# A recommender tower on one core: the first table rows on ScalarE's DMA queue, a later W2, a table-by-table low round in pass 1, and earlier holds for the gathers

## The reference

```python
e = jnp.stack([tbl_f[ids[:, f]] for f in range(26)], axis=1)           # 512 x 26 x 128
combined = jnp.concatenate([dense_features[:, None, :], e], axis=1)    # 512 x 27 x 128
interactions = jnp.einsum('bnd,bmd->bnm', combined, combined)
z = jnp.concatenate([dense_features, interactions[:, TRIU_I, TRIU_J]], axis=1)
h = jnp.concatenate([z, dense_features], axis=1)                       # 607 inputs
h = jnp.maximum(h @ W_top1 + b_top1, 0.0)                              # 512
h = jnp.maximum(h @ W_top2 + b_top2, 0.0)                              # 256
y = h @ W_top3                                                         # 512 x 1
```

## Time and profile before

| | |
|---|---|
| median of 3 runs | 121.35 us (120.82 to 123.39) |
| the profiled execution: its own time | 120.99 us |
| its span (first to last instruction) | 118.9 us |
| around the span | 2.09 us |
| PE busy, share of the span | 108.5 us, 91% |
| DVE, ACT, POOL busy | 85.0, 78.0, 57.3 us |

### The profile page before, as it was taken

How to read it: one execution, slowest core, us unless ns; L and a number is a source line. 1 busy time by engine, 2 the same in 40 slices (tenths; PEclk the granted TensorE clock), 3 DMA queues, 4 the chain that set the end, 5 groups by cost and what they waited for, 6 DMA issues and landing times.

```text
span 118.9 us, 2701 instructions
## 1 busy us (share of the span) xinstructions
PE 108.5 (91%) x1068; PEld 93.2 (78%) x1068; DVE 85.0 (71%) x171; ACT 78.0 (66%) x147; POOL 57.3 (48%) x66
## 2 busy tenths in 40 slices
PE   0079999999999999899999999999899999999993
PEld 0056787888888858558898999999789988999890
DVE  5779889999999957499959599582604981197002
ACT  4187838999999388599587699477504790178020
POOL 3777877787877777477740071078501700000000
PEclk9999999999999999999999999999999999999999
DMA  3899999692796924871210001001100000000000
GB/s 94 240 364 397 380 387 375 176 358 66 169 327 190 368 73 131 282 318 43 69 47 0 6 22 22 6 22 47 50 0 6 22 22 6 0 6 3 0 0 1
DMA packets 5582, 15.14 MB, mean 127 GB/s; under 512 B 1473, under 2 KB 1729, under 8 KB 5442
## 3 DMA queue, kind: packets, MB, share of 16 engines
q1 hardware_dynamic: 3890, 11.80, 28.0%
q0 software_dynamic: 1536, 3.15, 9.6%
q10 hardware_dynamic: 144, 0.02, 0.2%
HBM read 14.97 MB, written 0.00 MB: 126 GB/s over the span
## 4 chain that ended last, share of the span: by engine, by line
PE 70%; DMA 13%; ACT 8%; issue 3%; another core or an unknown queue 2%; DVE 1%; SPq 1%; ACTq 0%
PE dots_ps L712 13%; DMA table_raw<-picked_tables 13%; PE acc_ps L741 12%; PE dots_ps L628 10%; PE dots_ps L618 8%; PE turn_ps L757 5%; PE turn_ps L678 4%; PE acc_ps L651 3%; PE acc_ps L653 3%; PE acc_ps L732 3%; PE acc_ps L618 3%; PE acc_ps L628 3%; ACT z L382 2%; ACT cols L382 2%
## 5 line engine op out<-in xcount | busy, mean ns | idle before, releaser
L341 POOL DMA_INDIRECT rows<-tbl,ids_sb x48 | 53.5, 1114 | 16.6 <-issue 11.9
L515 DVE TENSOR_SCALAR onehot<-ids_row,row_number 128x1024 fp32r<-128x1024 int16 x49 | 33.6, 753 | 4.4 <-PE acc_ps L628 2.3
L359 DVE COPY z<-dots_ps 30x128 f32<-30x128 f32 (+5 forms) x80 | 21.0, 263 | 9.6 <-PE dots_ps L712 7.1
L382 ACT ACTIVATE z<-dots_ps 30x128 f32<-30x128 f32 (+5 forms) x80 | 19.7, 247 | 8.9 <-PE dots_ps L712 7.7
L382 ACT ACTIVATE table_hi<-table_raw 128x1024 fp32r<-128x1024 f32 (+1 forms) x16 | 15.2, 973 | 8.8 <-DMA table_raw<-picked_tables 6.8
L618 PE MATMUL acc_ps<-onehot,table_hi 128*128 128x512 f32 x52 | 14.4, 424 | 7.0 <-ACT table_hi L382 6.8
L618 PEld LDWEIGHTS acc_ps<-onehot,table_hi 128*128 128x128 f32 x52 | 10.2, 204 | 10.2 <-issue 6.8
L528 DVE TENSOR_TENSOR table_lo<-table_raw,table_hi 128x1024 fp32r<-128x1024 f32 (+1 forms) x16 | 17.1, 1114 | 1.2 <-ACT table_hi L382 1.2
L712 PEld LDWEIGHTS dots_ps<-cols 128*64 128x64 f32 x512 | 15.4, 138 | 1.1 <-issue 0.8
L712 PE MATMUL dots_ps<-cols 128*64 128x52 f32 x512 | 16.2, 222 | 0.0
L741 PE MATMUL acc_ps<-z,table_raw 128*128 128x128 f32 x128 | 15.3, 277 | 0.0
(11 more groups left out here) (48 smaller groups left out, 104.2 us busy)
## 6 DMA issues: line engine op xcount, KB each, us to landing
table_raw<-picked_tables SPq DMA_DIRECT2D x14, 512.0 KB
ids_row<-ids_picked SPq DMA_DIRECT2D x7, 256.0 KB
table_raw<-w SPq DMA_DIRECT2D x1, 1536.0 KB
rows<-tbl,ids_sb POOLq DMA_INDIRECT x48
w_sb<-w SPq DMA_DIRECT2D x1, 512.0 KB
table_raw<-picked_tables SPq DMA_DIRECT2D x2, 128.0 KB
dense_sb<-dense SPq DMA_DIRECT2D x1, 256.0 KB
ids_sb<-ids ACTq DMA_DIRECT2D x1, 24.0 KB, 2.5
```

The lines of the kernel that those rows point to most:

```text
L341: nc.gpsimd.indirect_dma_start(rows[:, t % GATHER_RING, n, :], None, tables[GATHERED[n]][:, :], index).then_inc(rows_in[t][g], 16)
L359: last = copy(z[QUAD * q:QUAD * q + rows_of, t % 2, :, QUAD * s + b0:QUAD * s + b1], src.rearrange("i b c -> i c b"))
L382: return nc.scalar.activation(dst, src, ACT.Copy)
L515: nc.vector.tensor_scalar(onehot[:, c], ids_row[:, pair % IDS_RING], row_number[first_row][:, c:c + 1], None, ALU.is_equal).then_inc(oneho ...
```

## The change

1. The two table loads of pass 0 go from SP's queue to ACT's, behind the ids of the gathers; SP's queue begins with ids row 0 and the tables of pass 1.
2. W2 and the last weights are issued behind W1 at the end of SP's list, and no longer behind the dense features near its start.
3. The memset of the unused columns of `cols` goes from DVE to Pool, ahead of Pool's first gather.
4. `lo_ready` counts once for each table, no longer once for each pass; all its waits are doubled. `LO_PIECE` goes, which alters no instruction.
5. In pass 1 PE's low round runs first over the eight chunks of table 0, as soon as that table's low part is there, and then over the eight of table 1; `chunk_done` is counted in the second half alone. In the other passes the two matmuls of a chunk stay together.
6. Pool's constants: the holds on `hi_used` stand at k = 17, 22, 27, 32, 37 (same counts 4, 5, 6, 7, 7), the memsets begin at k = 38, the pauses for `dots(0)`, `dots(1)`, `dots(2)` at k = 38, 40, 45, and `LANDED` follows.

```diff
-FREE_GATHERS = 20
+FIRST_FULL = 1
+FREE_GATHERS = 17
 GATHERS_A_PASS = 5
-LATE_GATHER = 39
+LATE_GATHER = 38
-PAUSES = {39: 0, 41: 1, 46: 2}
-LANDED = {0: 39, 1: 41, 2: 46}
+PAUSES = {38: 0, 40: 1, 45: 2}
+LANDED = {0: 38, 1: 40, 2: 45}
...
             load_ids_row(0)
-            load_tables(0)
-            load_tables(1)
+            load_tables(sp, 1)
             load_ids_row(1)
-            load_tables(2)
+            load_tables(sp, 2)
             sp.dma_start(dense_sb[:], dense).then_inc(dense_in, 16)
-            sp.dma_start(w2_sb[:], w2).then_inc(w2_in, 16)
-            sp.dma_start(last_sb[:], last_weights).then_inc(small_in, 16)
             for pair in range(IDS_RING, PAIRS):
                 p = FIRST_PASS[pair]
                 if p >= PASS_RING:
-                    sp.wait_ge(lo_ready, p - PASS_RING + 1)
-                    load_tables(p)
+                    sp.wait_ge(lo_ready, 2 * (p - PASS_RING + 1))
+                    load_tables(sp, p)
...
-            sp.wait_ge(lo_ready, NP - 1)
+            sp.wait_ge(lo_ready, 2 * (NP - 1))
             sp.dma_start(w1_sb, w1).then_inc(w1_in, 16)
+            sp.dma_start(w2_sb[:], w2).then_inc(w2_in, 16)
+            sp.dma_start(last_sb[:], last_weights).then_inc(small_in, 16)
...
+            nc.gpsimd.memset(cols[:, :, len(SLOT_NODE):SLOTS], 0.0).then_inc(cleared, 1)
             pool.wait_ge(ids_in, 16)
...
             act.dma_start(ids_sb[:], ids).then_inc(ids_in, 16)
+            load_tables(act, 0)
...
                     act.wait_ge(hi_used, p - 1)
-                    act.wait_ge(lo_ready, p - 1)
+                    act.wait_ge(lo_ready, 2 * (p - 1))
...
-            nc.vector.memset(cols[:, :, len(SLOT_NODE):SLOTS], 0.0).then_inc(cleared, 1)
...
                 for i in range(2):
-                    for c0 in range(0, n, LO_PIECE):
-                        part = slice(c0, min(c0 + LO_PIECE, n))
-                        last = nc.vector.tensor_tensor(table_lo[:, p % 2, i, part], table_raw[:, slot + i, part],
-                                                       table_hi[:, p % 2, i, part], ALU.subtract)
-                last.then_inc(lo_ready, 1)
+                    nc.vector.tensor_tensor(table_lo[:, p % 2, i, 0:n], table_raw[:, slot + i, 0:n],
+                                            table_hi[:, p % 2, i, 0:n], ALU.subtract).then_inc(lo_ready, 1)
...
-                pe.wait_ge(lo_ready, p + 1)
-                for c in ORDER[p]:
-                    for i in range(2):
-                        last = nc.tensor.matmul(sums[i], table_lo[:, p % 2, i, c, :], onehot[:, c, i, :],
-                                                start=False, stop=last_one and c == ORDER[p][-1])
-                    last.then_inc(chunk_done, 1)
+                def low(i, c):
+                    return nc.tensor.matmul(sums[i], table_lo[:, p % 2, i, c, :], onehot[:, c, i, :],
+                                            start=False, stop=last_one and c == ORDER[p][-1])
+
+                if p == FIRST_FULL:
+                    pe.wait_ge(lo_ready, 2 * p + 1)
+                    for c in ORDER[p]:
+                        low(0, c)
+                    pe.wait_ge(lo_ready, 2 * p + 2)
+                    for c in ORDER[p]:
+                        low(1, c).then_inc(chunk_done, 1)
+                else:
+                    pe.wait_ge(lo_ready, 2 * p + 2)
+                    for c in ORDER[p]:
+                        low(0, c)
+                        low(1, c).then_inc(chunk_done, 1)
```

More of the change, by code:

```diff
@@ L55 @@
 FIRST_PASS = [min(p for p in range(NP) if PASSES[p][0] == pair) for pair in range(PAIRS)]
-LO_PIECE = 8
 GATHERED = [f for f in range(NUM_TABLES) if f not in PICKED]
@@ L271, in build, with load_tables @@
         block = ctx.enter_context(nc.Block())
+        def load_tables(queue, p):
+            n = CHUNKS_OF[p]
+            for i in range(2):
+                slot = raw_slot(p) + i
+                r0 = 2 * P * CHUNKS_BEFORE[p] + i * P * n
+                src = picked_tables[r0:r0 + P * n].rearrange("(p c) d -> p c d", c=n)
+                queue.dma_start(table_raw[:, slot, 0:n], src).then_inc(table_in[slot], 16)
         @block.sync
@@ L276, in load_ids_row @@
                 sp.dma_start(ids_row[:, pair % IDS_RING], ids_picked[pair]).then_inc(ids_row_in[pair % IDS_RING], 16)
-            def load_tables(p):
-                n = CHUNKS_OF[p]
-                for i in range(2):
-                    slot = raw_slot(p) + i
-                    r0 = 2 * P * CHUNKS_BEFORE[p] + i * P * n
-                    src = picked_tables[r0:r0 + P * n].rearrange("(p c) d -> p c d", c=n)
-                    sp.dma_start(table_raw[:, slot, 0:n], src).then_inc(table_in[slot], 16)
             load_ids_row(0)
-            load_tables(0)
-            load_tables(1)
+            load_tables(sp, 1)
             load_ids_row(1)
-            load_tables(2)
+            load_tables(sp, 2)
             sp.dma_start(dense_sb[:], dense).then_inc(dense_in, 16)
-            sp.dma_start(w2_sb[:], w2).then_inc(w2_in, 16)
-            sp.dma_start(last_sb[:], last_weights).then_inc(small_in, 16)
             for pair in range(IDS_RING, PAIRS):
```

## The result

| | median, us | runs |
|---|---|---|
| before | 121.66 | 4 (120.82 to 123.39) |
| changed | 124.69 | 4 (123.57 to 125.64) |

The ratio is 1.0242, with an interval of 1.0127 to 1.0357: slower clear of noise, while the interval leaves open whether by more than 2 percent. All ratios and intervals here leave out the executions that were more than 1.5 percent above the fastest of their kernel, the medians do not. The forecast was 121.9, the range ended at 123.8. The profiled execution took 124.65 us, with a span of 122.9 against 118.9.

What follows compares the result with a forecast made beforehand. PE was taken as the bound, except for a load at the start. Span 118.9 + 0.55 (X) + 0.1 + 0.35 = 119.9, with 2.09 around it 122.0; forecast 121.9 us, range 119.4 to 123.8.

Steps and rivals of the forecast that it cites:

- late counts: Unexplained waits of DVE (2.3 us) and ACT (2.0) for PE's low-round counts, 36 to 56 us; carried unchanged.
- Rival 2: Pass 0 loads land no earlier and ACT's queue holds pass 1's copies: T 14.3, X +1.45, time 123.4 us; chance 0.15.
- T: End of PE's high round of pass 1, where its low round starts: 13.4 us forecast in place of 14.46.
- the split: Pass 1's table-by-table low round: first count 1.6 us later, one-hots of pass 2 at T + 2.44, X 0.55 later.
- X: End of DVE's low parts of pass 2, through which start gains reach the end: 22.85 us forecast against 22.31.
- DVE idle for over 2 us: Sign at the start: DVE idle this long ahead of the one-hots of pass 2, which start at 15.85 us.
- PE idle for 1 us ahead of its low round of pass 2: Sign: PE waits about 1 us for X, its low round of pass 2 starting near 23.1 us against 22.56.
- the second load of pass 0: On ACT's queue, forecast to land at 5.0 us, bounds 4.3 to 6.2, in place of about 6.25.
- rival 3: Late counts are accidental and the new holds remove them: -2.5 us, time 119.5, or 118.3 with rival 1; chance 0.15.
- The waits of the earlier trace: DVE's 2.3 us and ACT's 2.0 on PE's counts, 36 to 56 us; a change in size would show the forecast wrong.
- The tail's third gather: Three gathers behind `dots(2)`, no longer two, make PE wait and delay `dots(3)`: +0.35 us, 0 to +0.7.
- The gathers ahead of `dots(0)`: Under the new holds the last gather before the pause lands at 64.0 us, `dots(0)` at 64.63: +0.1, up to +0.6.

Runs made afterwards that it cites:

- after_again: The changed kernel unaltered, run again on chip A: median 121.09 us, 1.0196 (1.0148 to 1.0244) of the kernel before.
- before_few: The kernel before with 36 of 48 gathers left out, tiles 1 to 3 taking tile 0's rows: 117.07 us, 0.9628 of the kernel before.
- after_few: The changed kernel with the same 36 of 48 gathers left out: 119.76 us, 0.9867 of the kernel before.
- loads_only: The changed kernel with pass 1's low round chunk by chunk and the old gather holds (parts 1 to 4 remain): 119.76 us, 0.9895 of the kernel before.
- only_act_queue: The kernel before, with part 4, plus the loads of pass 0 on ACT's queue: 121.07 us, 0.9977 of the kernel before.
- before_again: The kernel before, with part 4 only, profiled once more on chip C: 120.23 us in one run.
- holds_on_loads: The changed kernel with pass 1's low round chunk by chunk, new gather holds kept: 121.43 us, 1.0101 of the kernel before.
- rows_on_sp: The changed kernel with the loads of pass 0 back at the head of SP's queue: 120.54 us, 1.0103 of the kernel before.
- before_profile: The changed kernel's source with all parts undone except part 4, profiled on chip B: 121.2 us in one run.

## Why the prediction was wrong

It named the mechanism of part 5, missed the sizes of three terms, all to the same side, and left out late counts as a cost. Rival 2 had T right (14.3, measured 14.35) and still fell short: its time was 123.4, and 124.69 came. In spans, 119.9 was forecast and 122.9 measured. Of these 3.0 us, 2.8 are there when the low round of pass 2 begins (25.87 against 23.1 forecast), 1.1 are won back by pass 6, and 1.1 and 0.3 are lost ahead of `dots(0)` and `dots(3)`. Two slips change nothing of this: 121.9 lies below 122.0 and 122.35 and not between them, and the count of the split is 2.31 behind T and not 2.44.

- **Right: X decides, and part 5 moves it.** The one-hots begin 2.31 us after the low round (T + 2.44 in the working) in the six profiles of the table-by-table round without a late count and without paired counts, and X follows 7.0 later (in `after_again` 24.6 after 17.56), as worked out. The split's price is in them all. DVE idle for over 2 us, PE idle for 1 us ahead of its low round of pass 2: both are in the profile.
- **The step that failed first: the size of T.** I took the second load of pass 0 at 5.0 and T at 13.4. It landed about 6.5, later than my worst bound of 6.2, PE started at 7.07, and T was 14.35. In the twelve profiles with the changed loads ACT's second copy starts between 6.42 and 7.89, in the eight with the rows on SP's queue between 4.48 and 6.42. With the second queue the rows did not come earlier, they came later, on each chip that has profiles of both. The rule that the Trainium skill states on its page "DMA: Bandwidth & Descriptors", section "Issuing engines are not separate DMA queues", pointed the right way, and I gave it 0.15. T - 13.4 is 0.95 us of the loss. The earlier loads of pass 1 were of no use either: with PE's start at 7.07 its eight matmuls of pass 0, 0.44 apart, fill PE until the high round starts at 10.62, and the copies were ready at 9.9.
- **The step that was missing: when a count arrives.** The sum had 0 for late counts, with rival 3 for their going away. They came in new places: 1.49 us ahead of the one-hots of pass 2 (3.80 after the low round and not 2.31), 0.56 behind the first of them, and 1.2 us ahead of `dots(0)`; from pass 2 to pass 6 the changed kernel was 1.1 us shorter. The waits of the earlier trace rows did change size (from 36 to 56 us DVE waits 1.3 us in all, ACT once for 3.0), which the prediction had named as a sign of being wrong. `before_few` and `after_few` agree with gathers as a condition: without the 36 neither has a late count. They don't prove it, for on chip A there was none either, with all 48 gathers. What makes counts late, and why they strike where they do, stays open.
- **The tail's third gather**: 0.66 measured, 0.35 forecast, 0.7 the bound. The gather went when I said (98.76, the third behind `dots(2)`, 2.9 us after the first of them), and landed later: the last move began at 101.76, 3.0 us after its issue, where I had 2.7. The other profiles give 0.65 to 0.7.
- **The gathers ahead of `dots(0)`**: 0.1 forecast with +0.6 as the bound, 1.2 measured. The landing itself was no trouble. The count of PE's turns was, and that wait was not on my list.
- **Parts 2, 3 and 4** at 0: `loads_only` contains them with part 1 and is 0.3 to 1.1 percent faster than before, so the four together cost nothing. No run takes them apart.
- **What the gain of `loads_only` may come from**, which no rival had: before can pause between pass 0 and pass 1, and then runs its high round at half pace. With the rows on ACT's queue PE starts at 6.9 to 8.4 and runs through, without a pause, in all twelve profiles of it. That is a mechanism that the profiles offer for the gain, and it is not shown. Part 1 alone was no faster clear of noise (`only_act_queue`, 0.9935 to 1.0019), before had no pause in `before_again` on the chip of the 0.9895, and no run separates the pause from the later W2 or from the earlier issue of pass 1's loads.

The version to keep is `loads_only`. On chip C it was faster than both kernels, clear of noise; on chip D it was 0.9967 of before, with an interval that reaches 1.0003. Both gains are under 2 percent.

## What to carry to other kernels

When a buffer is given back by a count, an earlier start that also delays the first count can lose more than it wins: ask for the reader's whole chain behind that count, not for the start. Test parts on more than one base, because here each bad part cost nothing that could be measured on the kernel before, and 0.85 and 1.3 percent on the version with the new loads. Where Pool's gathers are in flight, it is worth trying to place the last of them clear of the counts that other engines wait for: with the old holds that wait was 0.6 to 1.7 us, with the new ones 2.3 to 3.4, off chip A.

## What the runs showed of the hardware that was not expected

- Counts of PE can reach DVE and ACT up to 3.2 us late while PE goes on working (ACT's one-hot of pass 2 starts 6.60 us after the low round in the changed kernel, 3.37 in `after_few`), and two engines are then released at once: 61.80 and 61.86 us in `holds_on_loads`, 2.3 us after the issue of the last gather. In the changed kernel it was 2.1 (65.86 after 63.74). With 36 of 48 gathers left out there was none on the one chip tried, and on chip A there was none with all 48.
- A pause of PE of 0.7 to 2.0 us early in the program was followed by a round of 16 matmuls of 5.4 to 6.1 us in place of 3.7 to 4.9. In `rows_on_sp` the granted clock stood at 0.50 then, the 1.2 GHz level; in `before_profile` it was shown as 1.00 although the pace was the same, four matmuls in a microsecond and not six.
- The same kernel before had medians of 118.8 to 121.94 us on the five chips of the table, a spread larger than the effect of any one part.
